# A mixture-of-experts layer whose output rows are stored as tiles and gathered when combined

## The reference, cut to what matters

```python
adj = emb_s * emb_t * softmax(x) / sqrt(n)          # diagonal set to -inf
mask = zeros(n * n).at[top_k(adj.reshape(-1), 10240)].set(1.0).reshape(n, n)
scores = softmax(einsum('bsh,he->bse', mask, G))
value, indices = top_k(scores, 2)
w = einsum('bsk,bske->bse', value, one_hot(indices, 8))
gated = silu(mask @ gate_w[e].T) * (mask @ up_w[e].T)     # for each expert e
out = einsum('bsef,bse,ehf->bsh', gated, w, down_w)       # and a LoRA term
return x + out
```

## Time and profile before

| what | value |
|---|---|
| runs | 800.79 us median of 3 (798.49 to 806.63) |
| profiled execution | 801.54 us; its span 799.8 us |
| PE / PEld busy | 500.9 / 330.4 us |
| DVE busy | 523.6 us |
| ACT busy | 442.2 us |
| POOL busy | 389.5 us |
| mean granted clock of TensorE | 0.84 |
| DMA: q1 hardware, q0 software | 104.40 MB, 41.98 MB |

### The profile page before, as it was taken

One profiled execution on the slowest core, in us unless ns is written; L12 is line 12 of the kernel. 1 busy time (PEld: TensorE's weight loads), 2 busy tenths in 40 slices (PEclk: granted clock), 3 DMA queues, 4 the chain that ended last, 5 costly groups with the idle time before them and its releaser, 6 DMA issues.

```text
span 799.8 us, 13618 instructions
## 1 busy us (share of the span) xinstructions
PE 500.9 (63%) x3682; PEld 330.4 (41%) x3682; DVE 523.6 (65%) x1242; ACT 442.2 (55%) x655; POOL 389.5 (49%) x337
## 2 busy tenths in 40 slices
PE   0211187259878882788777717977669469788800
PEld 0200076146545551455445414544436246455400
DVE  5768789857598686776786867757872723343245
ACT  6687278738845476297445653973336345455300
POOL 7114200045366123588886136768971177877400
PEclk9755599669999895799999957998988869999865
DMA  9990060013312453368368733575478238767469
GB/s 317 360 269 0 3 261 28 0 49 113 113 74 91 166 217 107 125 226 283 133 220 272 299 102 131 206 261 175 169 252 326 94 102 287 262 207 260 164 259 381
DMA packets 76984, 147.29 MB, mean 184 GB/s; under 512 B 21475, under 2 KB 30699, under 8 KB 76400
## 3 DMA queue, kind: packets, MB, share of 16 engines
q1 hardware_dynamic: 59248, 104.40, 38.4%
q0 software_dynamic: 17664, 41.98, 14.7%
HBM read 95.47 MB, written 69.21 MB: 206 GB/s over the span
## 4 chain that ended last, share of the span: by engine, by line
DVE 20%; DMA 18%; issue 15%; POOL 14%; PE 13%; ACT 8%; DVEq 7%; SPq 2%; POOLq 1%; ACTq 0%
DMA put_rows<-y,where 5%; DMA piece<-put_rows 5%; DMA out_dram<-piece 5%; PE pa L690 4%; DVE mask L1075 4%; ACT mask L805 3%; POOL piece L538 3%; POOL xg L521 3%; DVE small L1037 3%; POOL piece L541 3%; DMA w<-put_rows 2%; ACT y L862 2%; DVEq L1364 2%; DVEq L1031 1%; DVE g_parts L1365 1%
## 5 line engine op out<-in xcount | busy, mean ns | idle before, releaser
L690 PE MATMUL pa<-w,xt 128*128 x1472 | 209.2, 296 | 5.4 <-issue 4.3
L862 ACT ACTIVATE y<-pc,where 128x512 f32<-128x512 f32 x184 | 121.7, 688 | 150.8 <-DMA put_rows<-y,where 94.6
L690 PEld LDWEIGHTS pa<-w,xt 128*128 128x128 f16 x1472 | 149.2, 102 | 74.1 <-issue 25.7
L529 POOL DMA_INDIRECT put_rows<-y,where x92 | 92.1, 1001 | 134.4 <-ACT y L862 114.0
L521 POOL DMA_INDIRECT xg<-mask_rows,where x92 | 99.1, 1078 | 115.8 <-DVEq L1349 95.0
L1357 DVE SCALAR_TENSOR_TENSOR g_full<-pa,where,s_act 128x144 f32<-128x144 f32 x92 | 33.5, 364 | 177.2 <-ACT s_act L854 177.2
L849 ACT ACTIVATE xt<-pb 128x1024 f16<-128x1024 uint8 x92 | 94.2, 1024 | 46.7 <-PE pb L677 46.5
L713 PE MATMUL pc<-wd,gt 128*128 x184 | 75.6, 411 | 13.1 <-ACT y L862 11.9
L714 PE MATMUL pc<-wd,gt 128*128 x184 | 75.9, 413 | 0.0
L715 PE MATMUL pc<-wd,gt 128*128 x184 | 75.5, 410 | 0.0
L716 PE MATMUL pc<-lb,gt 128*128 x184 | 75.5, 410 | 0.0
(11 more groups left out here) (208 smaller groups left out, 864.9 us busy)
## 6 DMA issues: line engine op xcount, KB each, us to landing
piece<-put_rows SPq DMA_DIRECT2D x96, 256.0 KB, 3.9
v<-in_x_dram SPq DMA_DIRECT2D x40, 512.0 KB, 8.5
piece<-in_x_dram SPq DMA_DIRECT2D x48, 256.0 KB, 2.9
out_dram<-piece SPq DMA_DIRECT2D x48, 256.0 KB
w<-put_rows SPq DMA_DIRECT2D x16, 512.0 KB, 9.6
w<-in_L_ffn_gate_w_dram SPq DMA_DIRECT2D x8, 512.0 KB, 10.3
w<-in_L_ffn_up_w_dram SPq DMA_DIRECT2D x8, 512.0 KB, 8.3
wd<-in_L_ffn_down_w_dram SPq DMA_DIRECT2D x8, 512.0 KB, 9.5
```

The lines of the kernel that those rows point to most:

```text
L529: pool.indirect_dma_start(out=put_rows[n % 2], out_offset=bass.IndirectOffsetOnAxis(ap=put_row[n][:, i:i + 1], axis=0), in_=y[:, g % NY, : ...
L690: last = pe.matmul(l1[g % 2], xt[:, g % 2, t, :], w1[:, bass.ds(e, 1), t, k, :].rearrange("p o n -> p (o n)"), start=(t == 0 and k == 0), ...
L862: nc.scalar.activation(y[:, g % NY, half * HALF:(half + 1) * HALF], pc[:, half, :], ACT.Copy, scale=y_scale[n][:, i:i + 1]).then_inc(y_rea ...
```

## The change

- y's tiles are stored by SP as they lie, 128 rows of 4 KB, to y_rows (23 x 128 rows for a batch): `store_tile`. ScalarE's y waits for y_stored instead of put. In SP's program store_tile(n, i-3) stands at tile i, behind store_piece, load_piece and, at tile 21, move_mask.
- To combine, POOL gathers for each of 16 (chunk, expert) pairs the 128 rows of y (512 KB) from y_rows into the one buffer piece[:, 2] (`gather_pair`), by pair_slot, and adds it over 1024 columns to the chunk of x (`add_pair`). Chunks of x are loaded and stored whole, by SP; two buffers. put_out and sum_piece are gone. In the last batch POOL does the 16 gathers into the weights' space, where SP did 16 loads.
- place_pairs keeps the pairs' slots as integers (pair_slot), and takes tile and place by a shift and a mask. It waits for pair_added (the pairs of the batch before the last) before it overwrites them.
- The split of the weights into three f16 parts, the token numbers and the power in vals are made by POOL (`split_weights`), behind pair_weighed; fill_table waits for split_ready.
- take_slots writes mask_row with its first instruction, which signals rows_ready; POOL's gathers wait for that, no longer for routed. The tokens' numbers are kept less S, so that an empty slot gives S, out of bounds.

The diff, cut:

```diff
-    PIECE_AT = {**{j + 1: j for j in range(9)}, **{j + 4: j for j in range(9, PIECES)}}
-    PIECES_FIRST = 14
+    PAIR_AT = {**{k: k for k in range(9)}, **{k + 4: k for k in range(9, Q)}}
+    ADD_AT = {i + 1: k for i, k in PAIR_AT.items()}
+    STORE_OUT_AT = {i + 2: k // ROLES for i, k in PAIR_AT.items() if k % ROLES}
+    LOAD_X_AT = {i + 1: c + NC for i, c in STORE_OUT_AT.items() if c + NC < C}
+    NEXT_X_AT = 21
...
+            def store_tile(n, i):
+                g = tile(n, i)
+                sp.wait_ge(y_ready, 2 * (g + 1))
+                if i == 0 and n >= 2:
+                    sp.wait_ge(pair_added, Q * (n - 1))
+                sp.dma_start(y_rows[n % 2][i * P:(i + 1) * P, :], y[:, g % NY, :]).then_inc(y_stored[g % NY], 16)
...
+                if n > 0:
+                    for c in range(NC):
+                        load_piece(n - 1, c)
+                for i in range(T):
+                    if n > 0 and i in STORE_OUT_AT:
+                        store_piece(n - 1, STORE_OUT_AT[i])
+                    if n > 0 and i in LOAD_X_AT:
+                        load_piece(n - 1, LOAD_X_AT[i])
+                    if n + 1 < B and i == NEXT_X_AT:
+                        move_mask(n + 1)
+                    if i >= BACK:
+                        store_tile(n, i - BACK)
...
+            def gather_pair(n, k):
+                u = Q * n + k
+                if u > 0:
+                    pool.wait_ge(pair_added, u)
                 pool.indirect_dma_start(
...
+                    out=piece[:, NC, :], out_offset=None, in_=y_rows[n % 2],
+                    in_offset=bass.IndirectOffsetOnAxis(ap=pair_slot[n][:, k:k + 1], axis=0),
+                    bounds_check=T * P - 1, oob_is_err=False).then_inc(pair_landed, 16)
+
+            def add_pair(n, k):
+                u, v_of = Q * n + k, C * n + k // ROLES
+                pool.wait_ge(pair_landed, 16 * (u + 1))
+                if k % ROLES == 0:
+                    pool.wait_ge(piece_landed[v_of % NC], 16 * (v_of // NC + 1))
+                else:
+                    pool.wait_ge(pair_added, u)
+                nc.gpsimd.tensor_tensor(piece[:, v_of % NC, :], piece[:, v_of % NC, :], piece[:, NC, :],
+                                        ALU.add).then_inc(pair_added, 1)
+
+            def split_weights(n):
+                pair = w_pair.rearrange("p (c r) -> p c r", c=C)
+                for r in range(ROLES):
+                    nc.gpsimd.tensor_copy(vals[:, :, r, 0], token_less)
+                pool.wait_ge(pair_weighed, n + 1)
+                nc.gpsimd.tensor_copy(vals[:, :, :, 4], power.unsqueeze(2).to_broadcast([P, C, ROLES]))
+                for k in range(PARTS):
+                    nc.gpsimd.tensor_copy(vals[:, :, :, 1 + k], pair)
+                    pool.drain()
+                    if k < PARTS - 1:
+                        nc.gpsimd.tensor_tensor(pair, pair, vals[:, :, :, 1 + k], ALU.subtract)
+                        pool.drain()
+                pool.sem_inc(split_ready, 1)
 
             for n in range(B):
-                pool.wait_ge(routed, n + 1)
+                pool.wait_ge(logits_ready, n + 1)
+                split_weights(n)
+                pool.wait_ge(rows_ready, n + 1)
                 pool.wait_ge(mask_stored, 16 * (n + 1))
...
                     if i + NX < T:
                         gather(n, i + NX)
-                    if i >= 3:
-                        put_out(n, i - 3)
+                    if n > 0 and i in ADD_AT:
+                        add_pair(n - 1, ADD_AT[i])
+                    if n > 0 and i in PAIR_AT:
+                        if PAIR_AT[i] == 0:
+                            wait_stored(n - 1)
+                        gather_pair(n - 1, PAIR_AT[i])
                     if n + 1 < B and i in BELOW_AT:
...
+                if n >= 2:
+                    dve.wait_ge(pair_added, Q * (n - 1))
                 V.tensor_reduce(slot.rearrange("p (c r) -> p c r", c=C), picked, AX.X, ALU.add)
...
+                V.tensor_copy(pair_slot[n], slot)
+                dve.drain()
+                V.tensor_scalar(slot_tile, pair_slot[n], SHIFT, None, ALU.arith_shift_right)
+                V.tensor_scalar(slot_in, pair_slot[n], P - 1, None, ALU.bitwise_and)
...
             def fill_table(n):
+                dve.wait_ge(split_ready, n + 1)
+                dve.drain()
...
+                V.tensor_scalar(mask_row[n], slots_ps[:, :, 0], float(S), None, ALU.add).then_inc(rows_ready, 1)
```

More of the change, by code:

```diff
@@ L129, in build @@
         y = sb("y", [P, NY, H], F32)
[L131 removed]
+        piece = sb("piece", [P, NC + 1, H], F32)
         gr_parts = sb("gr_parts", [P, HT, PARTS, E], BF16)
@@ L246, in build @@
         mask_row = [table_of(n, 0, I32) for n in range(B)]
-        put_row = [table_of(n, 1, I32) for n in range(B)]
+        pair_slot = [table_of(n, 1, I32)[:, 0:Q] for n in range(B)]
+        assert P == 1 << SHIFT
         g_scale = [table_of(n, 2) for n in range(B)]
@@ L276, in build @@
         mask_rows = [nc.dram_tensor(f"mask_rows{i}", [S, H], U8, kind="Internal").ap() for i in range(2)]
-        put_rows = [nc.dram_tensor(f"put_rows{i}", [ROLES * S, H], F32, kind="Internal").ap() for i in range(2)]
+        y_rows = [nc.dram_tensor(f"y_rows{i}", [T * P, H], F32, kind="Internal").ap() for i in range(2)]
         x_landed = [sem(f"x_landed{c}") for c in range(C)]
@@ L404, in _ @@
             for n in range(B):
-                more = n + 1 < B
-                if n == 0:
-                    move_mask(1)
-                else:
-                    if n == 1:
-                        sp.wait_ge(b_turned, 4)
-                        sp.wait_ge(a_turned, 1)
-                    wait_put(n - 1)
-                    for j in range(PIECES + NC):
-                        if j >= NC:
-                            store_piece(n - 1, j - NC)
-                        if j < PIECES:
-                            load_piece(n - 1, j)
-                        if more and j == PIECES_FIRST + NC - 1:
-                            move_mask(n + 1)
+                if n == 1:
+                    sp.wait_ge(b_turned, 4)
+                    sp.wait_ge(a_turned, 1)
+                if n > 0:
[10 more added lines that the diff above has]
+                        store_tile(n, i - BACK)
+                for i in range(T - BACK, T):
+                    store_tile(n, i)
                 if n + 2 < B:
@@ L426, in _ @@
             n = B - 1
-            wait_put(n)
-            for c in range(C):
-                for r in range(ROLES):
-                    sp.dma_start(last_put[c][r], put_roles[n % 2][r][:, c, :]).then_inc(rows_landed[c], 16)
             for c in range(C):
@@ L534, in sum_piece, with wait_stored @@
-            def sum_piece(n, j):
-                u = PIECES * n + j
-                at = u % NC
-                pool.wait_ge(piece_landed[at], 48 * (u // NC + 1))
-                nc.gpsimd.tensor_tensor(piece[:, at, 0, :], piece[:, at, 0, :], piece[:, at, 1, :],
-                                        ALU.add).then_inc(half_summed, 1)
-                pool.wait_ge(half_summed, u + 1)
-                nc.gpsimd.tensor_tensor(piece[:, at, 0, :], piece[:, at, 0, :], piece[:, at, 2, :],
-                                        ALU.add).then_inc(summed_piece, 1)
+            def wait_stored(n):
+                for i in range(NY):
+                    pool.wait_ge(y_stored[i], 16 * len(range(i, T * (n + 1), NY)))
@@ L561, in _ @@
                             below_third(n + 1, q)
-                    if n > 0 and i in PIECE_AT:
-                        sum_piece(n - 1, PIECE_AT[i])
-                for i in range(T - 3, T):
-                    put_out(n, i)
+            n = B - 1
+            wait_stored(n)
+            for c in range(C):
+                for r in range(ROLES):
+                    pool.indirect_dma_start(
+                        out=last_put[c][r], out_offset=None, in_=y_rows[n % 2],
+                        in_offset=bass.IndirectOffsetOnAxis(ap=pair_slot[n][:, ROLES * c + r:ROLES * c + r + 1],
+                                                            axis=0),
+                        bounds_check=T * P - 1, oob_is_err=False).then_inc(rows_landed[c], 16)
         @block.tensor
@@ L1344, in take_slots @@
                 V.tensor_scalar(y_scale[n], y_scale[n], y_unscale, None, ALU.mult)
-                V.scalar_tensor_tensor(none_here, none_here, -1.0, pair, ALU.add, ALU.add)
-                dve.drain()
-                V.tensor_copy(put_row[n], none_here)
-                V.tensor_tensor(mask_row[n], none_here, second_here, ALU.add)
                 dve.drain()
```

92 lines of the change are left out of this document (27 added, 65 removed).

## The result

| | before | after |
|---|---|---|
| runs, us | 799.64 median of 4 (798.4 to 806.63) | 943.46 median of 4 (940.37 to 945.7) |
| ratio | | 1.1775, 95% interval 1.1695 to 1.1855 |
| profiled execution, span | 801.54, 799.8 | 941.8, 940.1 |
| mean granted clock | 0.84 | 0.788 |

The account below looks back on a forecast made before the run. POOL's queue was taken to pace the stages, VectorE sharing the bound in batches 1 and 2. Router 0 -3.0, batches +3.4, +18.5, +11.0, last with tail +17.4: +47.3 on 801.54, 848.8, less 0.75 for the median: 848 us, range 815 to 878.

Parts of the forecast that it names:

- the ring takes 7.0 us: POOL's pair chain through one buffer: landing 4.2, add 2.45, gaps 0.35 us a round; bounds 5.6 to 8.
- the tail: Behind the last batch, POOL's 16 gathers replace loads; transfer-bound both times, so 0 lost, at worst +3 us.
- the 2.4 us that I had added for the diagonal: Batches 1 and 2: the diagonal stands before pair 2's add, so pair 3 goes out at T+31.2.
- The rounds of before: POOL's rounds in the kernel before the change, paced by its queue, taken as 5.8 us on the mean.
- rival C: Tile stores and pair gathers contend for DMA: 5.0 us to land, ring 7.8, 882 us in all; chance 0.12.
- Part 2: The pair chain on POOL: a round with a pair goes from about 5.8 to 7.0 us; last batch loses 17.4.
- Part 3: move_mask at tile 21: tile 18's store waits behind x and mask, line 1265 comes 24.5 us after x is issued.
- Part 1: The four routers between batches, with work cut or moved to POOL: each 3.0 us shorter, counting whole.
- Rival D: POOL's split of the weights is late, the table waits up to 3 us in each router: 860 us; chance 0.07.
- What was to show it: Signs: 7 us between pair gathers, POOL waiting 60 to 100 us, y's waits worst at tile 20, x later, routers 3.0 shorter.
- Rivals A and B: POOL's ring shorter. A: 5.7 us, 793 or 782 in all, chance 0.07. B: about 6.1, 810 to 815, chance 0.14.
- Rival E: Unseen slack before router or y hides half of the 33 us of batches 0 to 2: 832 us; chance 0.15.

Follow-up runs that it names:

- e_ring: Changed kernel with batches 0 to 2's loads of x into piece and stores to out made signals, tile stores of batches 2 and 3 cut to 64 KB: 878.6 us.
- e_noxo: Changed kernel without the loads of x into piece and the stores to out in batches 0 to 2, tile stores whole: 901.6 us.
- e_smally: Changed kernel with only the tile stores of batches 2 and 3 cut to 64 KB: 907.2 us.
- e_actq: Changed kernel with the tile stores issued on ScalarE's own queue right behind y, mask still moved at tile 21: 885.43 us.
- e_18: Changed kernel with only move_mask moved, to tile 18 instead of 21: 927.5 us.
- e_router: Kernel before the change with only the router's part of the change, puts and pieces as before: 799.96 us, ratio 0.9978.
- e_acc3: Changed kernel with accumulating gathers, three pieces in flight, tile stores on ScalarE's queue, mask behind the store of piece 5: 785.95 us, ratio to before 0.9793.
- e_acc18: Changed kernel with accumulating gathers onto the chunk of x, two pieces in flight, move_mask at tile 18, tile stores on SP: 838.5 us.

## Why the prediction was wrong, point by point

**The place of the loss was right, the size of one term was off.** The prediction called the pair chain a closed ring and put 42 rounds of it into the sum, each 0.1 us worth 4. The step that failed is "the ring takes 7.0 us". It measured 7.5 undisturbed (landing 4.35, the add 2.35, 0.77 to the next gather where I had allowed 0.35) and 8.8 to 9.4 on the mean. Of the excess over 42 rounds, some 20 us are the undisturbed ring's, nearly all of it that gap, and some 64 are the slower landings beside the burst, which the forecast left out. By stages, with the routers in them:

| | predicted | measured | difference | of it by the rounds |
|---|---|---|---|---|
| router 0 | -3.0 | -2.2 | 0.8 | |
| batch 0 | 3.4 | 1.0 | -2.4 | |
| batch 1 | 18.5 | 48.3 | 29.8 | 8 x 1.83 + 6 x 2.22 = 28 |
| batch 2 | 11.0 | 41.4 | 30.4 | 8 x 1.93 + 6 x 2.14 = 28 |
| batch 3, tail | 17.4 | 51.8 | 34.4 | 8 x 1.78 + 6 x 2.37 = 28 |

The last column takes all 14 rounds of a stage at their excess over 7.0. It carries 84 of the 93 us that were missing from 848.8. In batch 3 the tail, from the first of the last gathers on, takes 37.9 us instead of 33.5: another 4.4, where I had said 0, at worst 3. What else the column leaves out nearly cancels: the pause between pairs 8 and 9, which opens with a crowded landing, was some 4 us longer than forecast in each batch, and the 2.4 us that I had added for the diagonal lie within the rounds. The rounds of before, put at 5.8, are 5.65 on the mean; only the rivals used that.

**What made the ring long** was rival C's mechanism in a sharper form. C priced a mean contention (5.0 to land, 7.8 a round, 882 us). In fact the contention is timed by the kernel itself: the add's signal releases the next gather and SP's store of the piece, with three more transfers behind it, so every second gather meets 2 MB. e_ring shows it by taking the bytes away, e_noxo and e_smally by halves. What hid this is in Part 2, where I listed what queues behind SP's wait for pair_added (store_tile, move_mask) and priced it only as delay, not as a burst that comes out with the gather.

**Part 3** came out right in its length and not in its mechanism. x to the next first gather: predicted 36.6, measured 36.5, 36.3 and 37.8. I derived it from tile 18's store standing behind 5 MB, so that y 20 waits, and put the maxima of the late x at nothing. Only batch 2, after which no maxima are left to take, went that way: y 20 waited 21.34 us for the store, and e_actq, where no tile store stands there, is 4.0 shorter. In batches 0 and 1 VectorE stood 7.50 and 29.80 us for x, the gates behind it too, so that y 20 came late by itself and waited only 1.21 and 0.50 us more for its store. Timelines of SP, DVE and ACT of after (y 19 and y 20 of batch 1, y 20 of batch 2):

```profile
483.81 4.43 SPq L341 DMA_DIRECT2D v<-in_x_dram  x8
...
488.05 2.53 DVE L969 TENSOR_REDUCE small<-v 128x1 f32<-128x1024 f32 x2 [29.80 <-DMA v<-in_x_dram]
...
490.50 0.36 DVE L1365 SCALAR_TENSOR_TENSOR g_full<-pa,where,s_act 128x144 f32<-128x144 f32 x1
...
495.44 0.69 ACT L885 ACTIVATE y<-pc,where 128x512 f32<-128x512 f32 x1 [22.05 <-PE pc L739]
...
501.34 1.26 ACT L885 ACTIVATE y<-pc,where 128x512 f32<-128x512 f32 x2 [0.50 <-DMA y_rows<-y]
...
710.32 1.26 ACT L885 ACTIVATE y<-pc,where 128x512 f32<-128x512 f32 x2 [21.34 <-DMA y_rows<-y]
```

So two things that follow x end close together in batches 0 and 1, and e_actq, which takes one away, isn't shorter there at all (38.1 and 36.5); in its batch 1 VectorE still stands 23.10 us for x. That a path which I had put at nothing is as long as the one that I added up is luck. No run took away the other.

The prediction drew a rule from the Trainium skill ("DMA: Bandwidth & Descriptors", section "Queues, rings and completion order"): a queue's row is worked in order, and an engine takes turns between rows by the packet. e_18 agrees with the first half: in batch 0 y waited 12.77 us for a store behind x and mask. The turns did not save the gather. With nothing but a 128 KB gather of xg behind it in its own queue, it still landed with the third of the four transfers in SP's, after 8.5 us (761.96; the load of x issued at 755.41 landed after 6.8, at 762.2).

**Part 1** was near: predicted 3.0 a router, measured from the sum over the exponentials 2.9, 2.7, 1.5 and 2.4. Rival D (the split is late) is true for the last two, by 1.32 us of waiting, not 3; the second waits 0.24. What was gained there is worth little at the end (e_router).

**What was to show it:** POOL's wait for gathered pairs was expected at 60 to 100 us and is 175.8; ScalarE's waits at tiles 8, 16, 18 and 20 are there in batch 3 (8.24, 10.36, 9.44 and 10.00 us), and at tiles 2 to 7, 9, 15 and 17 too, which I hadn't named, with the longest of this batch at tile 6 (10.71) and not at 20; the first below_third came at T+90.7 in batch 1, not T+74.4; x went out at 274.46, 483.81 and 692.59 instead of 279.1, 454.9 and 615.8, the last two late by the rounds and the stages before them. **Rivals A and B** fell: no gather landed in under 4.1 us. **Rival E** may have had a little truth in batch 0, which lost 1.0 instead of 3.4; no run tests it.

**Where the 144 us went,** by the steps that undo them: tile stores out of SP's program 58; mask three tiles earlier on top of that 35; the ring opened and POOL's adds gone, with the mask still earlier (119 and 117 us behind the first gather), 65. Each is measured with the ones before it in place, and the middle one rests on a kernel that ran once. They add up to 158, the 144 and the 14 by which e_acc3 is below before.

## What to carry to other kernels

When a signal releases both a gather and another engine's queue of waiting DMAs, cost the gather with those bytes beside it, and look whether ready work piles up behind that queue's wait. A buffer that is single makes a latency count once for every use: measure the ring undisturbed and beside its own traffic, since the number of rounds multiplies the error. A store that only waits for its producer can go on the producer's queue; here that was worth 58 us.

## What was not expected of the hardware

- A gather of 512 KB in POOL's queue landed after 4.3 us with no burst beside it (the first of batch 3 in after) and after 8.5 beside 2 MB in SP's queue; an accumulating one after 6.5 and 8.2 (medians of e_acc18 and e_acc3, amid their other traffic).
- A POOL instruction of 16 elements a partition took 2.27 us instead of 0.23 beside VectorE's product of two tensors in SBUF over 2048 elements.
- From POOL's add to the indirect DMA that its signal releases it is 0.77 us, between indirect DMAs 0.30: in a ring or a full queue these gaps count.
